# First attention of a four-part network: the way from its outputs to the output projection, through on-chip transposes or through DRAM

## The reference

```
x = x + 0.5 * ffn0(layernorm(x))
x = x + attention0(layernorm(x))          # the part that is changed
x = x + 0.5 * ffn0(layernorm(x))
x = x + 0.5 * ffn1(layernorm(x))
x = x + attention1(layernorm(x))
x = x + 0.5 * ffn1(layernorm(x))

def attention0(x):                        # 16 heads of 8 columns
    q, k, v = split(x @ qkv_w + qkv_b)    # each (16 batches, 16 heads, 512, 8)
    a = softmax(q @ k.T * 8 ** -0.5)      # (16, 16, 512, 512)
    return concat_heads(a @ v) @ proj_w + proj_b
```

## Time and profile before

| what | value |
|---|---|
| median of 3 runs | 3264.02 us (3258.78 to 3268.07) |
| profiled execution, its own time | 3287.01 us |
| its span, first to last instruction | 3285.2 us |
| mean granted TensorE clock | 0.905 |
| PE busy | 2902.0 us, 88% |
| DVE busy | 2549.6 us, 78% |
| ACT busy | 1791.8 us, 55% |
| POOL busy | 919.2 us, 28% |

### The profile page before, as it was taken

One profiled execution on the slowest core, in us unless ns is written; L12 is line 12 of the kernel. 1 busy time (PEld: TensorE's weight loads), 2 busy tenths in 40 slices (PEclk: granted clock), 3 DMA queues, 4 the chain that ended last, 5 costly groups with the idle time before them and its releaser, 6 DMA issues. The chain is left out here.

```text
span 3285.2 us, 47363 instructions
## 1 busy us (share of the span) xinstructions
PE 2902.0 (88%) x15778; PEld 1773.0 (54%) x15778; DVE 2549.6 (78%) x6662; ACT 1791.8 (55%) x3223; POOL 919.2 (28%) x885
## 2 busy tenths in 40 slices
PE   6999879999999998999976698899899999989753
PEld 4666534444444443666644565566566656556432
DVE  7998768989989871899967898776476687697765
ACT  3544307778877774445445455464345555655444
POOL 2212121211211101122101555565233323434233
PEclk9999958999999996999985789899899999999965
DMA  4434322222212201344420000000000000000000
GB/s 130 101 83 104 81 98 95 76 77 95 86 67 95 83 25 52 79 104 94 89 52 1 1 14 20 13 26 20 33 10 11 14 14 7 14 7 26 7 7 26
DMA packets 71611, 167.26 MB, mean 51 GB/s; under 512 B 8792, under 2 KB 9416, under 8 KB 67144
## 3 DMA queue, kind: packets, MB, share of 16 engines
q1 hardware_dynamic: 69192, 160.04, 17.0%
q10 hardware_dynamic: 2176, 4.19, 0.3%
HBM read 120.68 MB, written 43.52 MB: 50 GB/s over the span
## 5 line engine op out<-in xcount | busy, mean ns | idle before, releaser
L697 DVE TENSOR_REDUCE att_mx<-att_s 128x1 f32<-128x512 f32 x1024 | 636.9, 683 | 92.6 <-PE att_s L949 91.7
L874 ACT ACTIVATE att_pt<-att_t 128x512 f32<-128x512 f32 x1024 | 548.5, 603 | 183.7 <-PE att_t L959 181.4
L949 PE MATMUL att_s<-att_k,att_q 32*128 32x512 f32 x1024 | 333.1, 532 | 31.2 <-DVE att_mx L697 16.0
L970 PE MATMUL att_o<-att_pt,att_vx 128*32 128x256 f32 x4096 | 335.8, 414 | 10.5 <-ACT att_oT L880 9.6
L959 PE MATMUL att_t<-att_q,att_k 32*128 32x512 f32 x1024 | 321.1, 521 | 2.9 <-ACT att_pt L874 2.6
L959 PEld LDWEIGHTS att_t<-att_q,att_k 32*128 32x128 f32 x1024 | 135.2, 190 | 217.5 <-ACT att_pt L874 106.5
L949 PEld LDWEIGHTS att_s<-att_k,att_q 32*128 32x128 f32 x1024 | 143.6, 194 | 69.8 <-DVE att_mx L697 51.3
L460 ACT ACTIVATE ffnA_h<-ffnA_up,b 128x512 f32<-128x512 f32 x144 | 98.6, 686 | 131.5 <-PE ffnA_up L105 131.0
L460 ACT ACTIVATE ffnB_h<-ffnB_up,b 128x512 f32<-128x512 f32 x144 | 98.6, 686 | 130.5 <-PE ffnB_up L105 130.0
L970 PEld LDWEIGHTS att_o<-att_pt,att_vx 128*32 128x32 f32 x4096 | 92.1, 112 | 143.4 <-ACT att_pt L874 70.3
L1896 ACT ACTIVATE att1k_sq<-att1k_k 128x512 f32<-128x512 f32 x128 | 76.1, 595 | 167.1 <-PE att1k_k L105 167.0
(11 more groups left out here) (535 smaller groups left out, 7710.7 us busy)
## 6 DMA issues: line engine op xcount, KB each, us to landing
ffnA_weights<-ffnA_weights SPq DMA_DIRECT2D x128, 256.0 KB, 5.3
att_q<-att_spread_q SPq DMA_DIRECT2D x16, 1024.0 KB, 5.0
att_k<-att_spread_k SPq DMA_DIRECT2D x16, 1024.0 KB, 4.8
att_spread_q<-att_qhi SPq DMA_DIRECT2D x32, 256.0 KB, 2.5
att_spread_k<-att_khi SPq DMA_DIRECT2D x32, 256.0 KB, 4.0
twk_hi<-ffnB_weights SPq DMA_DIRECT2D x32, 256.0 KB, 4.0
twk_lo<-ffnB_weights SPq DMA_DIRECT2D x32, 256.0 KB, 5.2
tgk_hi<-ffnB_weights SPq DMA_DIRECT2D x32, 256.0 KB, 6.1
```

What stands on the lines that cost most here:

```text
L697: v.tensor_reduce(top[b % 2][:, t, h + n % 2:h + n % 2 + 1], sbanks[n % 3][:, :], AX, ALU.max, negate=True).then_inc(mx, 1)
L874: a.activation(pt[k % 8][:, n % 2, :], tbanks[n % 3][:, :], ACT.Exp, scale=scale).then_inc(p_, 1)
L949: pe.matmul(sbanks[n % 3][:, :], qb[b % 3][r, u, t * P:(t + 1) * P], kb[b % 3][r, u, :], start=True, stop=True).then_inc(s_, 1)
L970: last = pe.matmul(obank[j * BLOCK:(j + 1) * BLOCK, cols], vxb[b % 3][:, t, 4 * u + j, :], pt[(2 * g + j // 2) % 8][:, j % 2, cols], start ...
```

## The change

The way out of the first attention goes through DRAM.

- Per unit, after ACT's copy, SP writes `att_oT` (256 KB) to a DRAM tensor `att_kept_o` (`outputs`). PE's `out`, DVE's `divided`, PE's `final` and ACT's `final` are gone.
- Per batch, SP reads the 16 rows of sums, spread over all 128 partitions of 64 numbers (`att_rec`), and the weighted values straight in the layout of the projection (`att_ocol`, 256 KB) (`gather`). DVE inverts the 64 columns once (`inverted_sums`, after the maxima of step 23). SP writes the inverses to DRAM, waits, and reads them back, each repeated for its head's 8 rows (`att_spread_rec`, 256 KB) (`invert`).
- POOL multiplies the two (`divided`, 128x512), behind the splitting of q and k in its program.
- On PE the projection v moves from step 17 to 21 and the output projection from 23 to 29; ACT's copy of v from 18 to 22; DVE's `ended` from 24 to 30.

The diff, cut to its core:

```diff
+INVERTED = 23
...
-    rec = mem.ring("rec", 2, [P, TILES, 4])
-    otok = mem.ring("otok", 2, [P, GROUP])
-    ocol = mem.sb("ocol", [P, GROUP])
+    rec = mem.sb("rec", [P, HEADS * GROUP // P])
+    ocol, spread_rec = mem.sb("ocol", [P, GROUP]), mem.sb("spread_rec", [P, GROUP])
...
+        def inverted_sums(b):                       # DVE
+            v.wait_ge(sums, 16 * (b + 1))
+            if b:
+                v.wait_ge(inverted, 16 * b)
+            v.reciprocal(rec[:, :], rec[:, :]).then_inc(inverse, 1)
...
-                if n == 8 and old:
-                    divided(UNITS * (m - 2) + 2)
-                if n == 16 and old:
-                    divided(UNITS * (m - 2) + 3)
+                if n == INVERTED and old:
+                    inverted_sums(m - 2)
...
-                if n == 24 and old:
-                    ended(m - 2)
-                if n == 26 and now:
-                    divided(UNITS * (m - 1))
...
-                if n == 31 and now:
-                    divided(UNITS * (m - 1) + 1)
+                if n == 30 and old:
+                    ended(m - 2)
...
+        def divided(b):                             # POOL
+            p.wait_ge(came, 16 * (b + 1))
+            p.wait_ge(divisor, 16 * (b + 1))
+            p.tensor_tensor(ocol[:, :], ocol[:, :], spread_rec[:, :], ALU.mult).then_inc(on, 1)
+
+        for m in range(-1, groups + 2):
+            if m + 1 < groups:
+                normal(m + 1)
+                spread(m + 1)
+            if m >= 2:
+                divided(m - 2)
...
+        def outputs(w):                             # SP
+            b, u = divmod(w, UNITS)
+            sp.wait_ge(oT, w + 1)
+            if u == 0 and b:
+                sp.wait_ge(came, 16 * b)
+                sp.wait_ge(sums, 16 * b)
+            sp.dma_start(kept_o[4 * u:4 * u + 4, :, :].rearrange("j r n -> (j r) n"), oTb[w % 2][:, :]).then_inc(kept[w % 2], 16)
+
+        def gather(b):
+            for written in kept:
+                sp.wait_ge(written, 16 * UNITS // 2 * (b + 1))
+            sp.dma_start(rec[:, :], kept_o[:, HDIM, :].rearrange("h (c n) -> h c n", c=P // HEADS)).then_inc(sums, 16)
+            if b:
+                sp.wait_ge(fp, b)
+            sp.dma_start(ocol[:, :], kept_o[:, 0:HDIM, :]).then_inc(came, 16)
+
+        def invert(b):
+            sp.wait_ge(inverse, b + 1)
+            if b:
+                sp.wait_ge(divisor, 16 * b)
+            sp.dma_start(kept_rec.rearrange("h (c n) -> (h c) n", c=P // HEADS), rec[:, :]).then_inc(inverted, 16)
+            sp.wait_ge(inverted, 16 * (b + 1))
+            sp.dma_start(spread_rec[:, :], kept_rec.unsqueeze(1).to_broadcast([HEADS, HDIM, GROUP])).then_inc(divisor, 16)
...
+            if old:
+                outputs(UNITS * (m - 2) + 2)
+            if new:
+                operand_q(m + 1)
+            if old:
+                outputs(UNITS * (m - 2) + 3)
+            if new:
+                operand_k(m + 1)
+            if old:
+                gather(m - 2)
+                invert(m - 2)
+            if now:
+                outputs(UNITS * (m - 1))
+                outputs(UNITS * (m - 1) + 1)
```

More of the change, by code:

```diff
@@ L599, in attn0 @@
     total = STEPS * groups
-    (var, root, normed, biased, xT, xc, qp, kp, qr, kr, ql, kl, vp, vx, s_, mx, mt, mT, mr, t_, p_, w_, oT, oTT, on,
-     fT, fc, fp, done) = signals(nc, ctx, name, "var root normed biased xT xc qp kp qr kr ql kl vp vx s mx mt mT mr t p w oT oTT"
-                                 " on fT fc fp done")
+    (var, root, normed, biased, xT, xc, qp, kp, qr, kr, ql, kl, vp, vx, s_, mx, mt, mT, mr, t_, p_, w_, oT, on,
+     fp, done) = signals(nc, ctx, name, "var root normed biased xT xc qp kp qr kr ql kl vp vx s mx mt mT mr t p w oT on fp done")
+    kept = signals(nc, ctx, name, "kept0 kept1")
+    came, sums, inverse, inverted, divisor = signals(nc, ctx, name, "came sums inverse inverted divisor")
     dq, dk, dm = [signals(nc, ctx, name, f"{n}0 {n}1 {n}2") for n in ("dq", "dk", "dm")]
@@ L633, in uses_of_misc @@
         yield from (("x", 0), ("q", 0), ("k", 0), ("v", 0))
-        for m in range(groups + 3):
-            new, old, now = m + 1 < groups, 2 <= m < groups + 2, 1 <= m <= groups
+        for m in range(groups + 2):
+            new, old, now = m + 1 < groups, m >= 2, 1 <= m <= groups
             if now:
@@ L639, in uses_of_misc @@
                 yield "x", m + 1
-            if old:
-                yield "out", UNITS * (m - 2) + 2
-            if new:
                 yield "q", m + 1
                 yield "k", m + 1
-            if old:
-                yield "out", UNITS * (m - 2) + 3
-            if new:
                 yield "v", m + 1
             if old:
-                yield "final", m - 2
                 yield "proj", m - 2
-            if now:
-                yield "out", UNITS * (m - 1)
-                yield "out", UNITS * (m - 1) + 1
     misc_uses = list(uses_of_misc())
@@ L672, in misc_free @@
                 pe.wait_ge(mr, k + 1)
[L673 to L676, removed]
             if kind == "proj":
@@ L709, in maxima @@
             v.tensor_tensor(rows[:, :, :, 1:8:2], tp, rows[:, :, :, 0:8:2].bitcast(F32), ALU.subtract).then_inc(mt, 1)
[L711 to L721, removed]
+        def inverted_sums(b):
[3 more added lines that the diff above has]
+            v.reciprocal(rec[:, :], rec[:, :]).then_inc(inverse, 1)
         def ended(b):
@@ L786, in normal @@
             p.tensor_tensor(xg(b), xg(b), A["pb"][:, :].unsqueeze(1).to_broadcast([P, TILES, C]), ALU.add).then_inc(biased, 1)
-        for b in range(groups):
-            normal(b)
-            spread(b)
+        def divided(b):
[8 more added lines that the diff above has]
+                divided(m - 2)
     def sync(sp):
@@ L825, in maxima @@
                 sp.dma_start(qb[b % 3][BLOCK * j + SUMMED:BLOCK * j + SHIFTED, :, :].bitcast(F32), spread_m[j, 0:2 * UNITS, :].rearrange("(u e) n -> e u n", e=2)).then_inc(dm[b % 3], 16)
-        operands(0)
-        for m in range(groups + 1):
-            if m:
-                maxima(m - 1)
-            if m + 1 < groups:
-                operands(m + 1)
+        def outputs(w):
[19 more added lines that the diff above has]
+            sp.dma_start(spread_rec[:, :], kept_rec.unsqueeze(1).to_broadcast([HEADS, HDIM, GROUP])).then_inc(divisor, 16)
+        operand_q(0)
+        operand_k(0)
+        for m in range(groups + 2):
+            new, old, now = m + 1 < groups, m >= 2, 1 <= m <= groups
+            if now:
+                maxima(m - 1)
+            if old:
[9 more added lines that the diff above has]
+                invert(m - 2)
+            if now:
+                outputs(UNITS * (m - 1))
+                outputs(UNITS * (m - 1) + 1)
     def scalar(a):
@@ L878, in out @@
             if w >= 2:
-                a.wait_ge(oTT, w - 1)
+                a.wait_ge(kept[w % 2], 16 * (w // 2))
             a.activation(oTb[w % 2][:, :], obank[:, :], ACT.Copy).then_inc(oT, 1)
[L882 to L886, removed]
         columns(0)
@@ L909, in scalar @@
                     raw_k(m + 1)
-                if n == 18 and new:
+                if n == 22 and new:
                     values(m + 1)
@@ L913, in scalar @@
                     out(UNITS * (m - 1))
-                if n == 22 and old:
-                    final(m - 2)
                 if n == 29 and now:
@@ L978, in maxima @@
             last.then_inc(mT, 1)
[L980 to L988, removed]
         def projected(b):
-            pe.wait_ge(fc, b + 1)
+            pe.wait_ge(on, b + 1)
             misc_free(pe, "proj", b)
@@ L1017, in tensor @@
                     turned(m + 1)
-                if n == 7 and old:
-                    out(UNITS * (m - 2) + 2)
                 if n == 9 and new:
@@ L1023, in tensor @@
                     project_k(m + 1)
-                if n == 15 and old:
-                    out(UNITS * (m - 2) + 3)
-                if n == 17 and new:
+                if n == 21 and new:
                     project_v(m + 1)
-                if n == 21 and old:
-                    final(m - 2)
-                if n == 23 and old:
+                if n == 29 and old:
                     projected(m - 2)
[L1032 to L1035, removed]
     with nc.Block() as block:
```

5 lines of the change are left out of this document (4 added, 1 removed).

## The result

| what | before | changed |
|---|---|---|
| median | 3262.47 us (4 runs) | 3329.23 us (3325.06 to 3332.84, 4 runs) |
| ratio to before | | 1.0203, 95% interval 1.0183 to 1.0223 |
| profiled execution (span) | 3287.01 us (3285.2) | 3332.84 us (3331.0) |
| mean granted clock | 0.905 | 0.891 |

The change makes the kernel 2% slower (1.8 to 2.2%), and 3330 was predicted. The medians differ by 67 us, the two profiled executions by 46: that of before lies 25 us above its median, that of the changed kernel 3.6.

A forecast was written before the change was run, and what follows sets the result against it. DVE's row of instructions bounds the batch, PE close behind. A batch: 44.7 + 4.0 + 4.1 + 0.5 = 53.3 us against 48.7; 13 batches +60, ends -2, 0, +9: +67 over the median 3264.02, said as 3330, range 3240 to 3375.

The forecast's parts named there:

- batch 15 and the start: Batch 15, with no read of k, gains the work removed; batch 1 gains only the divisions: -2 us together.
- tail up to ACT's last copy: In the tail seven transposings go, but also products that lifted the clock: called 0, within +-5 us.
- the very end: After ACT's last copy, transfers, inversion, product, projection and addition stand one after another: 14.3 us for 5.65, +8.7.
- Part 1: Work leaving DVE and PE per batch: 47.74 us falls to 44.7, 3.1 less, if nothing new is waited for.
- the 0.2 for the transposes there: Small wait behind the transposes of step 7 goes: -0.2 us per batch, by estimate.
- Part 2: At the inversion after step 23's maxima, DVE waits 4.0 us per batch for sums queued behind k's read.
- the bound from above: Upper bound on DVE's wait for the sums: 5.5 us, the queue filled also by late k writes.
- Part 3: DVE's wait leaves PE idle, so the clock falls every time from step 24 on: 4.1 us per batch, bounds 0 and 8.
- a fall there lasts until the projection: With no large PE product between steps 21 and 29, the lower clock stays until the projection in step 29.
- The premise that 1.36 us suffice: PE idle for 1.36 us was followed by the lower clock, so some 3 us idle should lower it every time.
- Part 4: DVE and POOL starting together at a batch's start: 0.5 us per batch charged, bounds 0 and 1.1.
- Rival 3: DVE reaches the inversion after the sums, so no wait: -46 us over 13 batches, 3225 us; chance 0.15.

The follow-up runs named there:

- e7: Changed kernel with outputs' write, sums' and columns' reads before q's read, inverses' write and read before k's, inversion at step 20 instead of 23: 3234.37 us, ratio 0.9901.
- e1: Changed kernel with only the sums' read moved, issued right behind the writes of k instead of behind k's 1 MB read: 3289.99 us, ratio 1.0079.
- e3: Changed kernel with the sums' read issued by ACT on its own queue at step 22, instead of by SP: 3308.67 us, ratio 1.014.
- e9: Changed kernel with 48 unread transposes of the identity added on PE behind its work of step 23: 3292.82 us, ratio 1.0082.
- e8: e7 with v's product moved back from step 21 to 17 and ACT's copy of v from 22 to 18: 3268.66 us, ratio 1.0005.
- e10: e8 with 8 unread transposes of the identity added on PE at step 21: 3242.82 us, ratio 0.9919.

## Why the prediction was right, and where not

The mechanism was right: the sums wait behind the read of k, DVE waits for them, PE idles and the clock falls. That 3330 lies within 1 us of the measured 3329 is luck. By spans, in which the sum was worked out, it gave +67 us and +45.8 were measured. The 23 us by which the profiled execution of before lay above its median were carried over to the changed kernel, whose profiled execution lies only 3.6 above its own. The two misses, of about 20 us each, cancelled. In us, by spans:

| term | predicted | measured |
|---|---|---|
| batch without new waits | 44.7 | 44.9 (52.8 - 5.25 - 2.65) |
| wait for the sums | 4.0 | 5.25 |
| fall of the clock | 4.1 | 2.65 |
| meeting of DVE and POOL | 0.5 | 0 |
| 13 batches against before | +60 | +50.4 |
| batch 15 and the start | -2 | -3.1 |
| tail up to ACT's last copy | 0 (+-5) | -9.4 |
| the very end | +8.7 | +8.0 |
| sum (with 0.1 less behind the attention) | +67 | +45.8 |

- **Part 1** held: 44.9, and 45.13 in e7. Of its pieces v's move measured 0.71 where I had 0.94, and the wait at step 7 stayed (1.45 us before and after), so the 0.2 for the transposes there was wrong. The inversion costs 0.40 at step 20 of e7.
- **Part 2** held in kind (e1, e7) and was 1.25 us too small: I charged 0.8 us for the write of outputs between q and k, and let the sums arrive 0.2 us behind k's 4.8 us. k's own writes landed 1.5 us later than before and the sums' 32 KB needed 6.3 us from their issue in the batch shown. The 5.5 that I gave as the bound from above was the nearer value.
- The rule of the Trainium skill that I weighed in Part 2 ("DMA: Bandwidth & Descriptors", Anatomy of one DMA: a fixed part and bytes over bandwidth) holds for the end, where the sums' read at 1332.30 released DVE at 1334.37, 2.07 us. In the batch it does not (6.3 us). There the sums came behind k, as the ring order has it (same page, Queues, rings and completion order), but that a common queue is the reason isn't shown: in e3 two queues met, and the small transfer was late all the same.
- **Part 3** failed in one step: "a fall there lasts until the projection". The clock came back in all 13 batches before the projection, the first full-array product, by 1.2 to 4.8 us, and 6.8 to 10.2 us after it fell. So step 27 cost less and step 29 nothing: 2.65 us, not 4.1. The row that the step rested on was read too narrowly. The low stretch around 520 us of the kernel before lasts only from 519.8 to 526.7 (with four transposes of the full array at 524.43), and the next product is at full clock:

```profile
526.98 0.53 PE L959 MATMUL att_t<-att_q,att_k 32*128 32x512 f32 x2
```

- That PE's idle time causes these falls is shown by e9. The premise that 1.36 us suffice holds only at times. The same meeting of DVE and POOL occurs three times in the kernel before, and in one the clock stays at 1.00 and the next product takes 0.50 us:

```profile
1022.05 0.50 PE L949 MATMUL att_s<-att_k,att_q 32*128 32x512 f32 x1 [1.36 <-DVE att_mx L697]
```

- **Part 4** was not there. In the changed kernel the 15 instructions take 277 ns in the mean; before, 483: 3 of the 15 last 1.35 us. None is left in the changed kernel, and in e7 one is back. That the later start of DVE took them away fits, but no run shows it.
- **The tail** was mis-sized: 36 transposes took 7.7 us of PE in it before, and up to ACT's last copy the clock is 0.69 without them, 0.66 with them. I had set what they save against a lower clock, and the clock didn't fall.
- The execution profiled of before holds four longer batches (51.5, 51.6, 49.5, 51.8), 13 us above undisturbed ones; an execution near the median may have fewer, which would bring the spans' 46 towards the medians' 67. There is no trace of one.
- **Rival 3**, no wait, needed DVE to come 4 us later or the read of k 4 us earlier. e7 reaches the same, by moving the sums ahead: its 3234 is 9 above the 3225 I gave for it.

## What to carry to other kernels

A small transfer on the critical chain is priced by what is in flight when it is issued, not by its size. Look at the whole chain, every write and read of it: issue its links ahead of the bulk reads that have slack, and leave room in the steps for a link that can't be. Moving one link only moves the wait. When a change takes large products out of a stretch of TensorE, ask what remains between the last one and the next: the low clock can cost more than the products did (here about 3 us a batch, against 1.09 us of transposes), and a product that has slack is best put into the thinnest stretch.

## What was not expected of the hardware

- A queue of its own didn't help by itself: 32 KB issued 0.17 us before a 1 MB read of another queue, or up to 0.37 us behind it, released DVE only 5.5 to 7.0 us after their issue (6 batches of e3); issued 0.22 us or more before it, 2.1 to 3.0 us (7 batches).
- The clock fell from 1.00 to 0.50 without an idle stretch of TensorE over 0.3 us (e8, 9 of 13 batches; the kernel before at 519.8 and 1066.0 us), and in e8's order 8 transposes of 1.09 us in all prevented it (e10). An idle stretch of 1.35 or 1.36 us was followed by the fall twice (728.1 and 970.4 us of the kernel before), and once it was not (1020.7).
- The clock rose again during steps of scores and `weigh` alone, 6.8 to 10.2 us after the fall, in all 13 batches of the changed kernel.
